# A graph-attention layer and a routed expert layer on one core: x + relu(h) - 1 formed by TensorE, expert weights loaded one by one, two blocks' rows sent between the last dispatches

## What is computed

```python
x = x + gnn(layernorm(x), adj)     # elu(softmax(mask(leaky_relu(e_src + e_dst))) @ (h @ W))
x = x + ffn(layernorm(x))          # 8 experts, the best 2 of each token
# ffn: h = relu(x @ W1[e].T + b1[e]); y = h @ W2[e].T + b2[e]; out += weight_of(e) * y
```

## Time and profile before

| | |
|---|---|
| median of 3 runs | 440.71 us (440.66 to 441.59) |
| the profiled execution | 442.13 us |
| its span, first to last instruction | 440.3 us |
| mean granted TensorE clock | 0.991 |
| busy, share of the span | PE 93%, DVE 82%, ACT 73%, POOL 66% |

### The profile page before, as it was taken

One profiled execution on the slowest core, in us unless ns is written; L12 is line 12 of the kernel. 1 busy time (PEld: TensorE's weight loads), 2 busy tenths in 40 slices (PEclk: granted clock), 3 DMA queues, 4 the chain that ended last, 5 costly groups with the idle time before them and its releaser, 6 DMA issues.

```text
span 440.3 us, 9161 instructions
## 1 busy us (share of the span) xinstructions
PE 407.3 (93%) x2272; PEld 308.3 (70%) x2290; DVE 358.9 (82%) x1410; ACT 321.3 (73%) x760; POOL 289.0 (66%) x292
## 2 busy tenths in 40 slices
PE   7998999889998888999999999999999999999980
PEld 3656666666666665688878888888888888876630
DVE  5689999999998898999887887777778778757683
ACT  2678887888888987688888678778767877866500
POOL 1041777777777777777777777767667657764662
PEclk9999999999999999999999999999999999999996
DMA  5995334333333344443632433322233233297888
GB/s 181 293 390 193 102 115 118 108 103 104 100 101 104 97 128 122 128 133 98 200 99 95 122 102 101 115 90 84 91 90 90 66 84 90 79 289 247 248 310 316
DMA packets 44004, 63.04 MB, mean 143 GB/s; under 512 B 7744, under 2 KB 24512, under 8 KB 43712
## 3 DMA queue, kind: packets, MB, share of 16 engines
q1 hardware_dynamic: 30448, 34.88, 26.5%
q0 software_dynamic: 9344, 20.10, 13.6%
q10 hardware_dynamic: 4176, 7.66, 5.3%
HBM read 27.28 MB, written 26.94 MB: 123 GB/s over the span
## 4 chain that ended last, share of the span: by engine, by line
PE 63%; DVE 20%; ACT 5%; DMA 5%; issue 4%; SPq 1%; POOL 1%; DVEq 0%; ACTq 0%; POOLq 0%
PE bank L1441 7%; PE bank L1455 7%; PE bank L1454 7%; PE bank L1457 7%; PE bank L1445 7%; PE bank L1442 7%; PE bank L1425 3%; PE bank L1433 3%; PE bank L1403 3%; PE bank L1316 3%; DVE xn L1066 3%; PE bank L1401 3%; DVE bn L901 2%; DVE neg_max L1048 2%; DVE score L1043 2%
## 5 line engine op out<-in xcount | busy, mean ns | idle before, releaser
L520 POOL DMA_INDIRECT expert_slots<-rows,slot_i x128 | 126.4, 987 | 55.4 <-issue 33.5
L712 ACT ACTIVATE yb<-bank,b_sb 128x512 f32<-128x512 f32 x36 | 24.8, 688 | 51.8 <-PE bank L1457 51.8
L1454 PE MATMUL bank<-hh,w_hi 128*128 128x512 f32 x144 | 60.1, 417 | 0.0
L1441 PE MATMUL bank<-xh,w_hi 128*128 128x512 f32 x144 | 58.5, 406 | 0.9 <-ACT xh L697 0.5
L1455 PE MATMUL bank<-hh,w_lo 128*128 128x512 f32 x144 | 57.4, 398 | 0.0
L1445 PE MATMUL bank<-xl,w_hi 128*128 128x512 f32 x144 | 56.9, 395 | 0.2 <-DVE xl L1122 0.2
L1457 PE MATMUL bank<-hl,w_hi 128*128 128x512 f32 x144 | 56.8, 395 | 0.3 <-DVE hl L1153 0.3
L1442 PE MATMUL bank<-xh,w_lo 128*128 128x512 f32 x144 | 56.8, 395 | 0.0
L536 POOL DMA_INDIRECT moe_rows<-hrelu,ysi x40 | 41.2, 1030 | 17.6 <-issue 10.7
L536 POOL DMA_INDIRECT moe_rows<-hexp,ysi x40 | 40.9, 1023 | 17.7 <-issue 10.1
L1146 DVE CAST hh<-z 128x512 fp32r<-128x512 f32 x36 | 16.5, 459 | 42.3 <-ACT z L702 41.9
(11 more groups left out here) (166 smaller groups left out, 1051.0 us busy)
## 6 DMA issues: line engine op xcount, KB each, us to landing
rows<-xn SPq DMA_DIRECT2D x32, 256.0 KB
xs<-expert_slots SPq DMA_DIRECT2D x27, 260.0 KB
x_all<-x SPq DMA_DIRECT2D x16, 256.0 KB, 3.5
w_raw<-w_t SPq DMA_DIRECT2D x2, 2048.0 KB, 13.7
w_raw<-moe_rows SPq DMA_DIRECT2D x16, 256.0 KB, 4.5
out<-x_all ACTq DMA_DIRECT2D x16, 256.0 KB, 4.7
xs<-expert_slots ACTq DMA_DIRECT2D x11, 260.0 KB
w_hi<-moe_rows SPq DMA_DIRECT2D x9, 256.0 KB, 4.1
```

Of the source, the lines that this page charges most:

```text
L520: nc.gpsimd.indirect_dma_start(out=slots, out_offset=bass.IndirectOffsetOnAxis(ap=slot_i[q][:, k * SUB + j:k * SUB + j + 1], axis=0), in_= ...
L712: nc.scalar.activation(yb[:, :], ps_y[:, :], ACT.Identity, bias=b2_sb[:, e:e + 1]).then_inc(yb_ok, 1)
L1441: nc.tensor.matmul(ps_h[c][:, :], w1_hi[:, e, chunk], xh[:, :], start=True, stop=False)
L1454: nc.tensor.matmul(ps_y[:, :], w2_hi[:, e, c, :], hh[:, c, :], start=c == 0, stop=False)
```

## The change

Four things change.

1. TensorE forms x + relu(h) - 1 in the bank of the attention (`elu_plus`: two matmuls with the identity in full precision and one in bf16, after z in its order, waiting for ScalarE's relu and exp). VectorE's `elu_sum` leaves the steps, and `residual_plus` adds min(exp(h), 1) to that bank. The eight fillers of `FILL_NORM` go, and the turn of the second norm moves ahead of wh. The last group, in `drain`, keeps the old form.
2. VectorE loses the three counts, the conversion of the expert numbers to floats (L951), and one of two additions to the variances. On ScalarE the first of four exponentials of the softmax moves to the end of the step before, and the copy of wh moves from there to behind the other three.
3. The weights are loaded by expert, 256 KB for each of the two products, after the `pass_on` of groups 0 to 7.
4. GpSimd sends the rows of block 0 after the dispatches of group 14, and those of block 1 between the two halves of the dispatches of group 15.

```diff
-            sp.dma_start(w1_raw[:, :, :], w1_t).then_inc(c_w1, 16)
-            sp.dma_start(w2_raw[:, :, :, :], w2_t).then_inc(c_w2, 16)
...
-            for q in range(2):
-                pass_on(0, q)
-            with sp.Fori(1, SURE_GROUPS // 2 + 1) as m:
-                for q in range(2):
-                    pass_on(m, q)
+            for g in range(SURE_GROUPS + 1):
+                pass_on(g // 2, g % 2)
+                if g < E:
+                    sp.dma_start(w1_raw[:, g, :], w1_t[:, g, :]).then_inc(c_w1, 16)
+                    sp.dma_start(w2_raw[:, g, :, :], w2_t[:, g, :, :]).then_inc(c_w2, 16)
...
+            def step(t, groups, q, m):
+                gr = groups[4]
+                if gr is not None:
+
+                    pool.wait_ge(slot_ok, gr + 1)
+                    pool.wait_ge(rowx_ok, 32 * (gr + 1))
+                    pool.sem_inc(stood, 1)
+                    dispatch(gr, 0, q)
+                    if gr == GROUPS - 1:
+                        send_rows(1, 1)
+                    elif t <= GROUPS:
+                        pool.wait_ge(prob_t_ok, t)
+                    dispatch(gr, 1, q)
+                    if gr == GROUPS - 2:
+                        send_rows(0, 0)
...
-            with pool.Fori(0, QUADS) as m:
+            for b in range(2, BUFS):
+                send_rows(b, b)
+            with pool.Fori(1, QUADS) as m:
...
                 if g1 is not None:
-                    softmax_exp(g1)
+                    softmax_exp(g1, range(1, SUB))
                 if isinstance(t, int) and 0 <= t - HIGH < 2:
                     high_halves(t - HIGH)
                 if g1 is not None:
+                    copy_wh(g1)
                     turned_prob(g1)
...
                 if g0 is not None:
-                    act.wait_ge(wh_ps, g0 + 1)
-                    nc.scalar.copy(wh[:, :, :], tiles(ps_wh)).then_inc(wh_ok, 1)
+                    softmax_exp(g0, range(1))
                 if gx is not None:
                     turned_norm(gx)
...
+            def residual_plus(gx):
+
+                dve.wait_ge(hexp_ok, gx + 1)
+                dve.wait_ge(plus_ps, gx + 1)
+                nc.vector.scalar_tensor_tensor(x_all[:, bass.ds(gx, 1), :, :].rearrange("p g s d -> p (g s) d"),
+                                               hexp[:, :, :], 1.0, tiles(ps_av), ALU.min, ALU.add).then_inc(x2_ok, 1)
...
-                nc.vector.tensor_copy(top_f[:, :, :], top_i[:, :, 0:2].rearrange("p t k -> p k t")).then_inc(topf_ok, 1)
-                dve.wait_ge(topf_ok, gl + 1)
...
-                if gx is not None:
-                    elu_sum(gx)
...
                 if gx is not None:
-                    residual(gx)
+                    residual_plus(gx)
                     second_stats(gx)
...
+            def elu_plus(g1):
+
+                pe.wait_ge(hrelu_ok, g1 + 1)
+                pe.wait_ge(hexp_ok, g1 + 1)
+                if not later(g1):
+                    pe.wait_ge(ones_ok, 2)
+                nc.tensor.matmul(ps_av[:, :], ident, x_all[:, g1, :, :].rearrange("p s d -> p (s d)"), start=True, stop=False)
+                nc.tensor.matmul(ps_av[:, :], ident, hrelu[:, :, :].rearrange("p s d -> p (s d)"), start=False, stop=False)
+                nc.tensor.matmul(ps_av[:, :], ident_b[:, :], minus_b[:, None, :].to_broadcast([P, SUB, P]), start=False, stop=True
+                                 ).then_inc(plus_ps, 1)
...
+                if g1 is not None:
+                    elu_plus(g1)
+                if gx is not None:
+                    if later(gx):
+                        pe.wait_ge(xn2_t_ok, gx)
+                    norm_turns(gx, q)
                 if g0 is not None:
                     if later(g0):
                         pe.wait_ge(wh_ok, g0)
...
                 if gx is not None:
-                    if later(gx):
-                        pe.wait_ge(xn2_t_ok, gx)
-                    fill(ps_t3, FILL_NORM)
-                    norm_turns(gx, q)
                     gates(gx, ps_gate)
```

More of the change, by code:

```diff
@@ L38 @@
 WARM_START, WARM_FIRST = 10, 8
-FILL_STEP, FILL_NORM = 3, 8
+FILL_STEP = 3
 FILL_EARLY, EARLY = 9, (1, 2)
@@ L101, in gnn_moe_kernel @@
         ones_b = sb("ones_b", [P, P], BF16)
+        minus_b = sb("minus_b", [P, P], BF16)
         log_v = sb("log_v", [P, BATCH, SUB])
@@ L137, in gnn_moe_kernel @@
         bn2 = sb("bn2", [P, SUB, 6])
-        mv2 = sb("mv2", [P, SUB, 2])
+        mv2 = sb("mv2", [P, 2, SUB, 2])
         var2 = sb("var2", [P, 2, SUB])
@@ L273, in gnn_moe_kernel @@
         hexp_ok = sem("hexp_ok")
+        plus_ps = sem("plus_ps")
         u_ok = sem("u_ok")
@@ L507, in _ @@
             pool.wait_ge(sure_out, 16 * SURE_BLOCKS)
[L509 to L525, removed]
             def send_rows(i, b, landings=()):
@@ L538, in send_rows, with dispatch @@
                         in_=ys[b][:, t, :], in_offset=None).then_inc(scattered[b], 16)
+            def dispatch(gr, k, q):
+                for j in range(SUB):
+                    nc.gpsimd.indirect_dma_start(
+                        out=slots, out_offset=bass.IndirectOffsetOnAxis(
+                            ap=slot_i[q][:, k * SUB + j:k * SUB + j + 1], axis=0),
+                        in_=rows[q][:, k, j, :], in_offset=None).then_inc(rows_out[q], 16)
+            def step(t, groups, q, m):
[12 more added lines that the diff above has]
+                        send_rows(0, 0)
+            by_steps(pool, step)
             def pool_sum(g):
@@ L574, in high_halves @@
             def high_halves(e):
-                act.wait_ge(c_w1, 16)
-                act.wait_ge(c_w2, 16)
+                act.wait_ge(c_w1, 16 * E)
+                act.wait_ge(c_w2, 16 * E)
                 nc.scalar.copy(w1_hi[:, bass.ds(e, 1), :].rearrange("p e h -> p (e h)"),
@@ L605, in softmax_exp, with copy_wh @@
                     act.wait_ge(prob_ps, g1)
-                for j in range(SUB):
+                for j in subs:
                     nc.scalar.activation(prob[:, j, :], score[:, j, :], ACT.Exp, bias=neg_max[:, j:j + 1],
                                          accum_out=psum_row[:, j:j + 1]).then_inc(exp_ok, 1)
+            def copy_wh(g1):
+                act.wait_ge(wh_ps, g1 + 1)
+                if later(g1):
+                    act.wait_ge(av_ps, g1)
+                nc.scalar.copy(wh[:, :, :], tiles(ps_wh)).then_inc(wh_ok, 1)
             def turned_prob(g1):
@@ L629, in elu_relu @@
                 if later(g1):
-                    act.wait_ge(u_ok, g1)
+                    act.wait_ge(x2_ok, g1)
                 for j in range(SUB):
@@ L685, in step @@
                     second_norm(gx, q)
+                if isinstance(t, int) and t + 1 < len(BATCHES):
+                    first_root(t + 1)
                 if g0 is not None:
-                    act.wait_ge(wh_ps, g0 + 1)
-                    nc.scalar.copy(wh[:, :, :], tiles(ps_wh)).then_inc(wh_ok, 1)
+                    softmax_exp(g0, range(1))
                 if gx is not None:
                     turned_norm(gx)
-                if isinstance(t, int) and t + 1 < len(BATCHES):
-                    first_root(t + 1)
             def round_x(i):
@@ L717, in drain @@
                 last = GROUPS - 1
-                softmax_exp(last)
+                softmax_exp(last, range(1, SUB))
+                copy_wh(last)
                 turned_prob(last)
@@ L792, in _ @@
             nc.vector.memset(ones_b[:, :], 1.0).then_inc(ones_ok, 1)
+            nc.vector.memset(minus_b[:, :], -1.0).then_inc(ones_ok, 1)
             nc.vector.memset(sure[:, 0:SURE], 2.0)
@@ L888, in residual @@
             def residual(gx):
-                dve.wait_ge(u_ok, gx + 1)
+                dve.wait_ge(u_ok, 1)
                 nc.vector.scalar_tensor_tensor(x_all[:, bass.ds(gx, 1), :, :].rearrange("p g s d -> p (g s) d"),
@@ L913, in second_var @@
                 dve.wait_ge(stats2_ok, gx + 1)
-                dve.sem_inc(met, 1)
                 for j in range(SUB):
-                    last = nc.vector.bn_aggr(mv2[:, j, :], bn2[:, j, :])
+                    last = nc.vector.bn_aggr(mv2[:, 0, j, :], bn2[:, j, :])
                 if norms(gx) > 1:
                     for j in range(SUB):
-                        last = nc.vector.bn_aggr(mv3[:, j, :], bn3[:, j, :])
+                        last = nc.vector.bn_aggr(mv2[:, 1, j, :], bn3[:, j, :])
                 last.then_inc(aggr2_ok, 1)
                 dve.wait_ge(aggr2_ok, gx + 1)
-                last = nc.vector.tensor_scalar(var2[:, 0, :], mv2[:, :, 1], EPS, None, ALU.add)
+                n = norms(gx)
+                nc.vector.tensor_scalar(var2[:, 0:n, :], mv2[:, 0:n, :, 1], EPS, None, ALU.add).then_inc(var2_ok, 1)
                 if norms(gx) > 1:
[L924 to L927, removed]
+                    nc.vector.tensor_copy(mean1[:, bass.ds(gx + AHEAD, 1), :].rearrange("p g s -> p (g s)"), mv2[:, 1, :, 0]
                                           ).then_inc(mean1_ok, 1)
```

(4 more changed lines are left out.)

12 lines of the change are left out of this document (3 added, 9 removed).

## The result

The changed kernel takes **445.01 us** (median of 5 runs, 444.94 to 447.69), the kernel before 440.71 (5 runs). The ratio is 1.0113, with a 95% interval of 1.0080 to 1.0145. Forecast were 441.6 us and a range up to 444.2, so the time lies 0.8 us above the range. The profiled execution took 445.0 us, with a span of 442.6 and a mean granted clock of 0.984 (0.991 before).

What follows compares the result with a forecast made beforehand. TensorE held 63% of the chain; graph steps ran through VectorE, TensorE and ScalarE, with GpSimd full. The lead is given back; block 8's rows 0.4 late plus 0.5 restart add 0.9: 440.71 + 0.9 = 441.6 us, range 438.6 to 444.2.

Steps and rivals of the forecast that it cites:

- the lead of the graph stage: Shorter graph-stage steps would let the expert stage begin 2.9 us earlier, bounds -2 and +5.4.
- lands at 227.5, 0.4 us later than TensorE used those rows before: Block 8's load, leaving at 224.8, would land at 227.5, against TensorE's earlier use of the rows at 227.16.
- the hole: Unexplained 1.85 us gap before a GpSimd dispatch at 188.07; half its excess was counted as gone, -0.8 us.
- SyncE's way: Time from the end of GpSimd's last dispatch until SyncE's queue is free for block 8's load: 6.25 us.
- The restart: After the wait in block 7, VectorE's order and SyncE's loop would cost 0.5 us, between 0 and 1.
- The clock: Rival: TensorE's clock falls to half while it waits in block 7, costing 2.0 us, total 443.6; chance 0.15.
- The steps: Graph-stage steps would shorten from 10.16 to 9.8 us, as rank starts about 0.36 earlier; bounds no gain and 0.5.
- hidden with 0.1 to spare: In each graph step the new matmuls, 1.96 us, would end 1.32 after the score; VectorE wants them at 1.42.
- The score of step 4: In the graph stage, this score, before at 40.94, would come 0.7 us later; bounds 0.4 earlier and 2.0 later.
- A credit of 0: Loading weights by expert would gain GpSimd's fifth dispatch 0, at most 0.19 us, as it waits for turned probabilities.
- Blocks 4 and 5 find their buffers free earlier: worth nothing: In the expert stage, earlier free buffers would gain 0, as no row showed VectorE waiting for one.
- The rival of dispatches that come in time: GpSimd's last dispatch ends before 216.8, so block 8's rows are not late; price about 438.8 us, chance 0.25.

Runs made afterwards that it cites:

- e1: The changed kernel with all of GpSimd's sends back behind the last dispatch; ratio 0.9956 to the kernel before.
- e2: The kernel before with only the sends of blocks 0 and 1 moved among the last dispatches; median 442.15 us, ratio 1.0026 to the kernel before.
- e4: The changed kernel with only block 0's four sends among the last dispatches, block 1's behind them; ratio 0.9953 to the kernel before.
- e3: The changed kernel with 21 filler matmuls on TensorE ahead of the turn of block 8's rows; ratio 1.0068 to the kernel before.
- e8: The changed kernel with 80 semaphore increments at the start of GpSimd's program; ratio 1.0145 to the kernel before.
- e7: e4 without the matmul that adds -1 to the residual; ratio 0.9977 to the kernel before.
- e5: e4 with 3 fillers instead of 12 in step 2 of the graph stage; median 438.96 us, ratio 0.9955 to the kernel before.
- e6: e4 with the weights loaded in two transfers ahead of the copied rows again; ratio 0.9958 to the kernel before.

## Why the prediction was wrong, step by step

The direction and the place were right: the sends ahead of the last dispatches make block 8's rows late, TensorE waits for them amid block 7 alone, and the lead of the graph stage is given back there (e1, e2 and e4 show it). **The step that failed is "lands at 227.5, 0.4 us later than TensorE used those rows before"**, whose terms were mis-sized (the hole and the sends in front of GpSimd's last dispatch above all), and with it the fall of the clock, which the sum left out.

- *The late rows.* They were turned at 229.66, 2.50 later than before instead of 0.4. The excess is made of GpSimd's last dispatch, 220.33 instead of 218.6, and of the load, 229.66 - 226.34 = 3.32 from its issue to the turn instead of 2.7 (the end of its traffic; where an engine waits for block 8's rows, the traces have 3.0 to 3.3); SyncE's way took 6.01 instead of 6.25. Against the kernel before, GpSimd's fifth dispatch was 0.65 later (forecast 0.5), the hole 0.30 longer (forecast 0.8 shorter), and the sends took 11.25 (forecast 10.2; even the bound of 11.0 was too low), while the other dispatches took 0.53 less. Counting half of the hole as gone, an error of 1.1, and the sends, 1.05, were the largest: the hole stood at the same dispatch in all ten traces, with 1.85 to 2.24 us.
- *The restart.* Forecast 0.5. From block 8's turn to block 9's are 6.76 before, and where the rows were late and the clock held 7.16 (e3), 7.27 (e2) and 7.47 (e8): 0.4 to 0.7.
- *The clock.* Its fall costs 1.42 us by e3 and 1.11 by e8; it was priced at 2.0 with a chance of 0.15. TensorE's own work lost 2.1, close to that price, but the forecast left out that at full clock TensorE has to wait again a little later. That the price came close is luck: the ten first matmuls, which it was taken from, stand in stretches whose granted clock is 1.00 (0 to 6 us), so the row does not show half clock. The forecast expected an idle time of 3 to 4 us and gave the fall little chance. Two programs that are alike in the expert stage show both outcomes: a wait of 2.98 left the clock at full (e8), one of 4.92 brought it to half (the changed kernel). The length of the wait alone does not part them, as the clock of the changed kernel fell at about 227.3, some 2.6 us into its wait; what does is not shown. The Trainium skill ("TensorE: Matmul & The Clock Gate", "Part 1: The HAM clock gate") says that activity is what releases the throttle. The changed kernel's trace agrees with it inside the expert stage: the clock fell to 0.50 while TensorE was idle, and showed 0.96 again in the stretch from 234, after TensorE had worked from 229.66 on.
- *Together:* 2.50 + 0.40 + 1.42 = 4.32 at block 9's turn, or 2.50 + 0.71 + 1.11 by e8; the forecast had 0.4 + 0.5. That the median rose by nearly the same, 4.30, is in part chance, since the two traces end only 2.3 apart.
- *The steps.* Forecast 9.8, measured 9.87. The new matmuls, "hidden with 0.1 to spare", take 2.12 instead of 1.96 and end late enough to be on the chain; e7 gives 9.66 without one of them. The score of step 4 came 1.16 later instead of 0.7 (within its bounds): the step from the second score to the third took 10.23 instead of 8.63, and 8.92 in e5, so the fillers behind the new matmuls make most of it. So the lead was 2.05 instead of 2.9. The length of the steps did not move the end, since the rows of block 8 decide and GpSimd cannot follow; the late score of step 4 did, by the 0.65 by which GpSimd's fifth dispatch came later.
- *The weights.* A credit of 0 was right (e6).
- *"Blocks 4 and 5 find their buffers free earlier: worth nothing"* was wrong. With the shorter steps VectorE waits for such a buffer: 3.90 in e1's profiled execution, 0.74 in e4, 1.38 in e5 and 2.33 in e7. This fits that four early sends do no harm against none (0.9953 and 0.9956): what they cost at block 8's rows they may save at that buffer, which no run takes apart.
- *The rival of dispatches that come in time* needed the last one before 216.8. e4, at 215.15, meets it and shows what it gives, 0.47%; the changed kernel was 3.5 us away from it.

## What to carry to other kernels

When work is put ahead of something that another engine needs, add up the whole queue to the moment of need and take the slack after the rest of the change: shorter steps had used up 2 of it here, four sends still fitted (e4), and eight cost 11.25 us and turned a gain of 0.4% into a loss of 1.1%. A wait of TensorE can have a second price, the fall of its clock: here waits of 1.17 and 2.98 us left it at full and one of 4.92 did not, which cost 1.1 to 1.4 us more. A stall that the profile explains by nothing, but that stands at one dispatch, should be counted in full until a run shows it gone.

## What was not expected of the hardware

- The clock stayed at 0.50 for over 4 us after TensorE had work again: the turn began at 229.66, the stretch from 232 to 234 was still at 0.50, and that from 234 showed 0.96.
- GpSimd takes up to 2.5 us more or less for the same work from one execution to another: from the fifth dispatch to the last its 132 transfers take 220.33 - 47.72 = 172.61 us in the changed kernel's trace and 217.87 - 47.74 = 170.13 in e8's. Single ones take 1.4 to 1.5 us instead of 0.96. What they meet there was not tried. It may well be what parts e8's execution of 441.74 us from those of 445 or more, but only the first has a trace.
- The hole of 1.85 to 2.24 us ahead of the 114th dispatch is there in every kernel, is not moved by 80 more instructions ahead of it, and has no releaser in the profile.
